# Bounded window row ids, and one wait less on the sync queue, in a fused attention and expert kernel on one Trainium2 core

## What is computed

```python
h = (x_flat @ W_gat).reshape(M, HEADS, NUM_EXPERTS)        # M = 16384 nodes
src = jnp.concatenate([edge_index[0], loops]); dst = jnp.concatenate([edge_index[1], loops])
e = jax.nn.leaky_relu(a_src[src] + a_dst[dst], negative_slope=0.2)
e_max = jax.ops.segment_max(e, dst, num_segments=M)
ee = jnp.exp(e - e_max[dst])
denom = jax.ops.segment_sum(ee, dst, num_segments=M)
agg = jax.ops.segment_sum(h[src] * (ee / (denom[dst] + 1e-16))[:, :, None], dst, num_segments=M)
scores = _layernorm(agg.reshape(M, 16) + b_gat, ln_gamma, ln_beta).reshape(M, HEADS, NUM_EXPERTS).mean(1)
# top 2 of 4 experts by scores, softmax over them, out = sum of w[e] * (gelu(x @ W1[e] + b1[e]) @ W2[e] + b2[e])
```

## Time and profile before

| | us |
|---|---|
| median of 3 runs, no profiler | 3323.31 (3321.15 to 3329.72) |
| span of the profiled execution | 3908.9 |
| of it up to the first window gather | 2011.7 |
| 30 turns, from the first window gather of turn 0 to that of turn 30 | 1823.8 |
| the rest | 73.4 |

### The profile page before, as it was taken

The page is one execution under the profiler, slowest core; times in us unless marked ns, Lnnn a source line. Parts: engine busy times, 40 slices in busy tenths (PEclk is TensorE's granted clock), DMA queues, the critical chain, the costliest instruction groups (busy, mean ns, idle before and its releaser), DMA issues. The chain is left out here.

```text
span 3908.9 us, 31732 instructions
## 1 busy us (share of the span) xinstructions
PE 1964.9 (50%) x9058; PEld 1350.2 (35%) x9113; DVE 2118.6 (54%) x4420; ACT 1188.0 (30%) x2437; POOL 1852.3 (47%) x1785
## 2 busy tenths in 40 slices
PE   0777742377777426676232445345244433444446
PEld 0666641255454215666211122122122212222223
DVE  7799887997789984444312334333233323433336
ACT  0676753244344204554201212112121111221212
POOL 5000247354444214445675555654655665556552
PEclk9988855699898657776556666666666666766668
DMA  6970001011111021001111111111111111111111
GB/s 212 345 292 1 17 26 34 22 35 47 34 44 30 31 84 38 17 21 22 41 28 32 28 31 37 26 34 27 32 30 31 37 26 34 27 38 33 28 31 38
DMA packets 172773, 197.65 MB, mean 51 GB/s; under 512 B 60217, under 2 KB 127072, under 8 KB 172032
## 3 DMA queue, kind: packets, MB, share of 16 engines
q1 hardware_dynamic: 107184, 118.69, 9.1%
q0 software_dynamic: 60160, 67.73, 8.4%
q10 hardware_dynamic: 5328, 9.97, 0.7%
HBM read 96.94 MB, written 105.25 MB: 52 GB/s over the span
## 5 line engine op out<-in xcount | busy, mean ns | idle before, releaser
L1453 POOL DMA_INDIRECT edge_rows<-node_table,edge_ids x1024 | 990.2, 967 | 687.3 <-POOLq L1193 385.9
L1581 PE MATMUL x_b_hid<-x_featT,x_w 128*128 128x512 f32 x512 | 353.6, 837 | 599.8 <-PEq L1193 395.7
L1096 POOL DMA_INDIRECT token_results<-arena,token_of x160 | 247.2, 1545 | 370.3 <-ACT arena L1030 271.4
L1581 PEld LDWEIGHTS x_b_hid<-x_featT,x_w 128*128 128x128 f32 x512 | 113.1, 254 | 830.7 <-issue 635.6
L1109 POOL DMA_INDIRECT adjacent<-keys,row_ids x256 | 243.0, 949 | 315.5 <-DVE counts L785 168.1
L1588 PE MATMUL x_b_res<-x_w,x_hid 128*128 128x128 f32 x2048 | 311.2, 304 | 146.1 <-issue 146.1
L1089 POOL DMA_INDIRECT slots<-arena,send x128 | 169.7, 1325 | 433.5 <-ACT arena L987 398.7
L1588 PEld LDWEIGHTS x_b_res<-x_w,x_hid 128*128 128x128 f32 x2048 | 275.9, 212 | 245.6 <-issue 245.4
L1415 DVE SCALAR_TENSOR_TENSOR x_weighed<-x_b_res,gates,x 128x128 f32<-128x128 f32 x128 | 36.1, 344 | 523.5 <-DVEq L1193 493.0
L562 DVE TENSOR_TENSOR sort_ping<-sort_pong 128x1024 f32<-128x1024 f32 (+1 forms) x184 | 285.8, 1594 | 47.5 <-ACT sort_pong L973 43.5
L562 DVE TENSOR_TENSOR sort_pong<-sort_ping 128x1024 f32<-128x1024 f32 (+1 forms) x184 | 285.7, 1594 | 37.0 <-ACT sort_ping L973 33.3
(11 more groups left out here) (333 smaller groups left out, 4303.3 us busy)
## 6 DMA issues: line engine op xcount, KB each, us to landing
edge_table<-zeros SPq DMA_DIRECT2D x8, 5120.0 KB
edge_rows<-node_table,edge_ids POOLq DMA_INDIRECT x1024
arena<-slots SPq DMA_DIRECT2D x40, 260.0 KB
slots<-zeros SPq DMA_DIRECT2D x2, 5120.0 KB
edge_table<-edge_rows SPq DMA_DIRECT2D x64, 160.0 KB
out_dram<-x_y ACTq DMA_DIRECT2D x33, 256.0 KB
adjacent<-in_adj_dram SPq DMA_DIRECT2D x32, 256.0 KB, 2.8
arena<-token_results SPq DMA_DIRECT2D x32, 256.0 KB
```

The costliest lines, as they stand in the source:

```text
L1096: pool.indirect_dma_start(rows_dram, bass.IndirectOffsetOnAxis(token_of[:, n % 4, r:r + 1], 0), res[:, n % 2, r, :], None, bounds_check=TO ...
L1453: pool.indirect_dma_start(rows[:, u, c, :], None, table_dram, bass.IndirectOffsetOnAxis(ids[:, u, c:c + 1], 0)).then_inc(rows_in[u], 16)
L1581: pe.matmul(b_hid[:, c % 2, :], w1[:, c // HC1, c % HC1 * P:(c % HC1 + 1) * P], featT[:, :], start=True, stop=True).then_inc(hid_mm, 1)
```

## The change

Two edits, in `edges_and_experts1` alone:

```diff
+        stored = sb("stored_rows", [P, 1])
...
-            dve.tensor_copy(win_ids[:, :], first_edge[:, 0:UNIT]).then_inc(picked, 1)
+            dve.tensor_scalar(win_ids[:, :], first_edge[:, 0:UNIT], float(BLOCK + PART - WINDOW), None, ALU.min).then_inc(picked, 1)
             link(dve.tensor_copy(left[:, 0:GRAPHS], degree[:, :]))
             dve.sem_inc(planned, 1)
+            link(dve.memset(stored[:, :], float(BLOCK + PART - WINDOW)))
...
                 came()
-                dve.sem_inc(win_seen, 1)
...
                 step(dve.tensor_reduce(newtop[:, :, :], by_head, AX_X, ALU.max))
                 step(dve.tensor_tensor(first_edge[:, mine], first_edge[:, mine], adv[:, :], ALU.add))
+                step(dve.tensor_scalar(stored[:, :], stored[:, :], float(BLOCK), None, ALU.add))
                 settle()
                 step(dve.tensor_tensor(newtop[:, :, :], newtop[:, :, :], top[:, mine, :], ALU.max))
-                dve.tensor_copy(win_ids[:, :], first_edge[:, after]).then_inc(picked, 1)
+                dve.tensor_scalar(win_ids[:, :], first_edge[:, after], stored[:, 0:1], None, ALU.min).then_inc(picked, 1)
...
-            def pass_on(part, u, turn, windows_read):
+            def pass_on(part, u, turn):
                 sp.wait_ge(rows_in[u], turn * (16 * PART_TILES))
                 sp.dma_start(ids[:, u, :], ids_v[bass.ds(part + 2, 1)].rearrange("o q c -> q (o c)")).then_inc(ids_in[u], 16)
-                if windows_read:
-                    take(sp, win_seen, 1)
                 sp.dma_start(edges_v[bass.ds(part, 1)].rearrange("o q f -> q (o f)"), rows[:, u, :, :].rearrange("p c w -> p (c w)")).then_inc(rows_out[u], 16)
```

More of the change, by code:

```diff
@@ L1167, in edges_and_experts1 @@
         ids_in, rows_in, rows_out = ([sem(f"e_{n}{u}") for u in (0, 1)] for n in ("ids_in", "rows_in", "rows_out"))
-        picked, win_in, win_late, win_clear, win_seen, win_free = (sem(f"w_{n}") for n in (
-            "picked", "in", "late", "clear", "seen", "free"))
+        picked, win_in, win_late, win_clear, win_free = (sem(f"w_{n}") for n in (
+            "picked", "in", "late", "clear", "free"))
         step_s, scored, exped, gap_s, gap_exped = (sem(f"w_{n}") for n in ("step", "scored", "exped", "gap", "gap_exped"))
@@ L1491, in _ @@
                 sp.dma_start(to[:, :], across(a[of], GAT)).then_inc(consts_in, 16)
-            def pass_on(part, u, turn, windows_read):
+            def pass_on(part, u, turn):
                 sp.wait_ge(rows_in[u], turn * (16 * PART_TILES))
                 sp.dma_start(ids[:, u, :], ids_v[bass.ds(part + 2, 1)].rearrange("o q c -> q (o c)")).then_inc(ids_in[u], 16)
-                if windows_read:
-                    take(sp, win_seen, 1)
                 sp.dma_start(edges_v[bass.ds(part, 1)].rearrange("o q f -> q (o f)"), rows[:, u, :, :].rearrange("p c w -> p (c w)")).then_inc(rows_out[u], 16)
             for u in (0, 1):
-                pass_on(u, u, 1, False)
+                pass_on(u, u, 1)
             sp.wait_ge(planned, 1)
@@ L1504, in _ @@
             with sp.Fori(0, more) as t:
-                pass_on(t * 2 + 2, 0, t + 2, False)
-                pass_on(t * 2 + 3, 1, t + 2, True)
+                pass_on(t * 2 + 2, 0, t + 2)
+                pass_on(t * 2 + 3, 1, t + 2)
             for u in (0, 1):
```

## The result

The changed kernel takes 3338.64 us (median of 5, 3332.78 to 3342.74), the kernel before beside it 3322.34 us (3317.78 to 3329.72). The ratio is 1.0050, with a 95% interval of 1.0038 to 1.0061: slower by 16 us, where I had forecast no change.

The account below looks back on a forecast made before the run. POOL's issue of indirect DMAs, 45.0 us a turn, was taken to bound the kernel. The terms 0 + 0 + 0 + 0.2 on 3323.3 gave about 3323 us, with a range of 3270 to 3340.

Parts of the forecast that it names:

- What bounds the kernel: Last layer's loop: without the profiler POOL's issue of 36 indirect DMAs sets a turn, 45.0 us; other engines fit in.
- The wait for `win_seen`: SP's wait ahead of its store: 14.8 us of slack in an undisturbed turn, so removing it is worth 0.
- The store that meets the windows: Slower rival: early store delays window gathers by up to 2.7 us a turn, 84 us at most; slower in all 0.08.
- The new operations on DVE: One small operation (0.16 us) and a minimum replacing a copy, ahead of `picked` each turn: cost 0, conditionally up to 16 us.
- POOL beside DVE: POOL's gathers slowed beside the new DVE operation: at most 0.16 us a turn, 5 us in all; taken as 0.
- The mean of 967 ns: Mean of 1024 gathers beside DVE's small operations, used as evidence that the new operation slows POOL by 0.
- The silences as a cost of recording: All engines but POOL fall silent in most turns; read as profiling cost, explaining a span 585.6 us above the median.
- The rival "faster": DVE is late without the profiler too, so the removed wait frees POOL: 3242 us, or 3302 if partly true; chance 0.19.
- turn 19's 58.2 us: A profiled turn without a store wait, 2.6 us under the mean of 60.8, taken as the gain each turn: 81 us.
- The rule that I weighed: Tensor-scalar operations on DVE can block GpSimd's port for the whole instruction: some 5 us higher, 3328; by the rows 0.
- The signs: Expected in the changed profile: store within 1 us of ids' DMA, gather waits below 60 us, window waits 300 or more.
- DVE's 16 us on a condition: New DVE operations cost up to 31 x 0.5 = 16 us if DVE starts on its windows later than 22.3 us.

Follow-up runs that it names:

- e6: Kernel before with SP's store held back until DVE has read the windows, not just until they are in; 3319.09 us, ratio 0.9999.
- e15: Changed kernel with DVE's signal left in and nobody waiting for it; 3334.46 us, ratio 1.0028 to the kernel before.
- e17: Kernel before with the bound on window row ids alone, signal and SP's wait kept; 3330.29 us, ratio 1.0010.
- e2: Kernel before with the bound on window row ids alone, signal and SP's wait kept, in a silent session; ratio 1.0137.
- e10: Kernel before with the bound on window row ids alone, signal and SP's wait kept, again in a silent session; ratio 1.0148.
- e16: Kernel before with the bound on window row ids alone, signal and SP's wait kept, once more in a silent session; ratio 1.0119.
- e4: Changed kernel as it is, in a silent session; 3985.50 us against 3881.19 for the kernel before, ratio 1.0267.

## Why the prediction was wrong

- **What bounds the kernel: right.** POOL sets the turn in clear executions, its waits vanish, the other engines fit in. A turn is 45.9 us for the kernel before (e6 in its place), not 45.0; the 0.9 are the holds, which in 30 turns are 27 us.
- **The wait for `win_seen`: right at 0.** e6 put 10 us on top of it, and the time stayed within 0.1%. The store that now goes out ahead of DVE is another matter: e15 against e17 has 0.16 us a turn beside it, which stays open.
- **The store that meets the windows.** It does, 1.8 us into the turn instead of my 1.4, and takes 3.5 us instead of 1.8. DVE does not start later by it (7.52 us in e15, 7.54 in e17), so the path by which I let it cost something, windows that come in late, is not what happened.
- **The new operations on DVE, "Cost 0", and POOL beside DVE, "I take 0": this is the step that failed.** The change costs 0.43 us a turn (46.34 against 45.91), 12.9 us in 30 turns, all of it in holds of POOL's gathers. The new operations' time on DVE is hidden, as I said. What I missed is that on DVE everything ahead of a large operation sets where it falls among POOL's gathers. The term had only the new operation's own 0.16 us as a possible hold ("32 x 0.16 = 5 us"); the row that I had for it, a gather of 1.36 us beside the 128x1536 multiply, was the real mechanism, and I used it as a price for the wrong operation: no gather starts inside the new ones. The bound's 0.10 us more ahead of the subtraction is worth 0.12 us a turn. I also dismissed the removed signal in one clause, as an instruction that goes. Its going costs 0.15 us a turn. The other 0.16 come with the early store and are unexplained.
- **The mean of 967 ns as evidence for 0: wrong step.** 967 - 944 = 23 ns on each of 1024 is 24 us of holds in that profile, in the very row that I cited. I should have asked what they depend on.
- **The silences as a cost of recording, absent from the times: wrong as stated.** The kernel has executions at 3890 us. My median came from clear ones and my profile from a silent one, and 585.6 us between them was a reason to doubt that the two belong together, not only to look for a place to put the difference.
- **The rival "faster": wrong in sign.** Where DVE is late, the change costs 2.7%, against 1.2 to 1.5% for the bound alone with the wait kept (e2, e10, e16), so the removed wait and signal gain nothing there; I took turn 19's 58.2 us as what every turn would be, but that turn follows one with a pause.
- **The rule that I weighed, and its neighbour.** From the Trainium skill (SBUF — State Buffer, Who interferes with whom) I took the sentence on tensor-scalar operations. The same section of the Trainium skill says that a DVE instruction with two SBUF inputs contends with a GpSimd instruction that reads SBUF. The traces agree with it: all 462 held gathers of the clear turns meet tensor_tensor and scalar_tensor_tensor operations with two operands in SBUF, and the tensor_reduce of 2.7 us and the operation that reads PSUM hold none.
- **The signs.** The store follows its ids' DMA within 1 us, and POOL's waits ahead of the gathers fell under 60 us (27.1), as forecast. A gather of over 1.25 us from start to start beside the new operation was to be a sign of being wrong; no gather starts inside the new operation, and the longer ones sit beside the large ones. POOL's waits ahead of the windows did not grow to 300 us in the clear profile (13.0), and did in the silent e4 (573.0), where the span grew against the kernel before instead of falling.
- **The range** (3270 to 3340) took in 3338.64 by luck: its upper end was added up from 5 us of holds by the new operations' own time and half of DVE's 16 us on a condition that did not come about.

## What to carry to other kernels

Where POOL's indirect DMAs set the pace, an operation on DVE, which idles half the time, is still not free: look at the gathers that are longer than their median and what runs beside them, and cut the operations that hold them into pieces. An edit that moves such an operation by 0.1 us can cost more than the wait that it removes gains. And where a profile and a median differ by 18%, ask first whether they are of the same kind of execution. In the silent kind this change, which takes out a wait of 385 us, made the kernel slower by 2.7%.

## What the runs showed of the hardware

- An indirect gather of 128 rows takes 0.94 us on POOL and the next one starts 0.30 us later. One that starts 0.05 us or more into a DVE operation with two SBUF operands ends 0.82 us after that operation if this is later, up to 2.24 us in all; one that starts 0.04 us or less into it is not held.
- A `tensor_reduce` of 2.7 us and a `scalar_tensor_tensor` with one operand in PSUM held no gather, in 360 and 314 cases.
- A store of 160 KB issued beside the window gathers took 3.5 us to land, and 1.8 us behind them.
- A held gather gets in between two queued DVE operations: beside pieces of about 0.5 us it took 1.11 us.
- A signal of its own on DVE moves what follows by 0.08 us (7.44 to 7.52 as a mean of 30 starts; five of them, 7.86).
- One program ran at 3322 and at 3890 us, by the session; why is not shown.
